# Causal mask of the row maxima on the diagonal: one TensorE matmul and a plain maximum in place of a masked VectorE pass

## What is computed

```python
xn = _layernorm(x)                                   # x: (1, 2048, 256)
k, q, v = einsum('ihd,bpd->biph', W_K / W_Q / W_V, xn)   # 16 heads of 128
scores = einsum('biph,biqh->biqp', k, q)
mask = tril(ones((pos, pos)))
masked = scores * mask - 1e10 * (1.0 - mask)
attn = softmax(masked / sqrt(128), axis=-1)
z = einsum('biqp,biph->biqh', attn, v)
s = einsum('df,bqf->bqd', W_O, z_flat)
g = silu(ffn(xn))            # base linear layer and one of 8 low-rank experts for each token
out = x + s * g
```

## Time and profile before

| | |
|---|---|
| median of 3 runs | 1450.78 us (1450.16 to 1451.8) |
| the profiled execution | 1450.27 us, its span 1448.2 us |
| PE busy | 1412.4 us, 98% of the span |
| DVE busy | 1191.9 us, 82% |
| ACT busy | 1086.5 us, 75% |
| POOL busy | 829.3 us, 57% |
| chain that ended last | PE 94% |

### The profile page before, as it was taken

The page is one execution under the profiler, slowest core; times in us unless marked ns, Lnnn a source line. Parts: engine busy times, 40 slices in busy tenths (PEclk is TensorE's granted clock), DMA queues, the critical chain, the costliest instruction groups (busy, mean ns, idle before and its releaser), DMA issues.

```text
span 1448.2 us, 23330 instructions
## 1 busy us (share of the span) xinstructions
PE 1412.4 (98%) x7788; PEld 1197.4 (83%) x7788; DVE 1191.9 (82%) x2541; ACT 1086.5 (75%) x2260; POOL 829.3 (57%) x688
## 2 busy tenths in 40 slices
PE   5899999999999999999999999999999999999996
PEld 4688888888888888888888888888888888888775
DVE  6679897798878987788977988789887898779964
ACT  2578886878778787788868787787877888688842
POOL 3265674556566474656745566555746567455840
PEclk9799999999999999999999999999999999999998
DMA  2110001010100101100010001001011000100002
GB/s 80 30 30 16 13 10 45 8 19 12 30 23 9 23 9 30 30 16 10 14 44 9 15 16 30 23 8 23 8 31 30 16 8 16 38 11 16 16 30 87
DMA packets 30072, 33.75 MB, mean 23 GB/s; under 512 B 11009, under 2 KB 17665, under 8 KB 29953
## 3 DMA queue, kind: packets, MB, share of 16 engines
q1 hardware_dynamic: 29952, 32.26, 9.3%
HBM read 30.02 MB, written 2.23 MB: 22 GB/s over the span
## 4 chain that ended last, share of the span: by engine, by line
PE 94%; DVE 2%; POOL 1%; DMA 1%; ACT 1%; issue 1%; SPq 0%; POOLq 0%; DVEq 0%; ACTq 0%
PE ps L293 27%; PE ps L294 26%; PE ps L295 26%; PE ps L745 9%; PE ps L780 3%; PE ps L757 1%; POOL colsum L446 1%; DMA acc<-x_dram 1%; DVE p_lo L577 1%; PE ps L808 1%; PE ps L698 0%; DVE acc L569 0%; PE ps L714 0%; DMA spread<-max_dram 0%; ACT p_hi L525 0%
## 5 line engine op out<-in xcount | busy, mean ns | idle before, releaser
L446 POOL TENSOR_TENSOR colsum<-colsum,probs 128x512 f32<-128x512 f32 (+3 forms) x512 | 643.6, 1257 | 240.6 <-ACT probs L524 208.0
L577 DVE TENSOR_TENSOR p_lo<-probs,p_hi 128x512 fp32r<-128x512 f32 (+3 forms) x640 | 561.9, 884 | 5.4 <-ACT p_hi L525 3.1
L524 ACT ACTIVATE probs<-ps 128x512 f32<-128x512 f32 (+3 forms) x640 | 344.8, 539 | 207.7 <-PE ps L295 123.3
L501 ACT ACTIVATE ps<-maxrow 128x512 f32<-128x512 f32 (+3 forms) x640 | 354.1, 553 | 0.0
L525 ACT ACTIVATE p_hi<-ps 128x512 fp32r<-128x512 f32 (+3 forms) x640 | 344.7, 539 | 0.0
L592 DVE TENSOR_REDUCE partmax<-ps 128x1 f32<-128x512 f32 x384 | 254.3, 681 | 7.6 <-PE ps L745 7.6
L293 PE MATMUL ps<-qT_hi,kT_hi 128*128 128x512 f32 (+3 forms) x640 | 239.7, 375 | 3.7 <-ACT ps L501 3.5
L293 PE MATMUL ps<-p_hi,v_hi 128*128 128x512 f32 (+3 forms) x640 | 238.0, 372 | 1.8 <-DVE p_lo L577 1.8
L294 PE MATMUL ps<-qT_lo,kT_hi 128*128 128x512 f32 (+3 forms) x640 | 233.3, 365 | 0.0
L295 PE MATMUL ps<-p_hi,v_lo 128*128 128x512 f32 (+3 forms) x640 | 233.1, 364 | 0.0
L295 PE MATMUL ps<-qT_hi,kT_lo 128*128 128x512 f32 (+3 forms) x640 | 232.8, 364 | 0.0
(11 more groups left out here) (107 smaller groups left out, 2247.1 us busy)
## 6 DMA issues: line engine op xcount, KB each, us to landing
spread<-max_dram SPq DMA_DIRECT2D x64, 256.0 KB, 3.8
wraw<-wqk_dram SPq DMA_DIRECT2D x16, 256.0 KB, 4.1
acc<-x_dram SPq DMA_DIRECT2D x4, 512.0 KB, 7.2
wraw<-wv_dram SPq DMA_DIRECT2D x8, 256.0 KB, 4.8
wraw<-wo_dram SPq DMA_DIRECT2D x8, 256.0 KB, 3.4
probs<-x_dram SPq DMA_DIRECT2D x4, 512.0 KB, 4.6
out_dram<-acc SPq DMA_DIRECT2D x4, 512.0 KB, 3.0
max_dram<-rowmax SPq DMA_DIRECT2D x64, 2.0 KB, 1.4
```

What stands on the lines that cost most here:

```text
L446: nc.gpsimd.tensor_tensor(total[:, c0:], total[:, c0:], tile[:, c0:], ALU.add)\
L501: nc.scalar.activation(st[job.n % SCORE_BANKS][:, c0:], maxrow[:, job.g, c0:], ACT.Copy)\
L524: nc.scalar.activation(probs[:, k, c0:], src, ACT.Exp, scale=SCALE).then_inc(probs_ready, 1)
L577: nc.vector.tensor_tensor(p_lo[:, k, c0:], probs[:, k, c0:], f32(p_hi[:, k, c0:]), ALU.subtract)\
```

## The change

The masked pass is replaced. On TensorE, after the matmul of a diagonal row maximum, a bfloat16 matmul with `mask_bf` stationary and `ident_bf` moving adds the transposed triangle to the last 128 columns of the bank, and the semaphore `aux_full` is raised by it and not by the matmul ahead of it. On VectorE every row maximum is now the same plain `reduce_max`, over the `w` columns where it is diagonal. The memset, the custom pass, its accumulator read, the tiles `mask_rows` and `wait_slot` and the view `masked_row` go, and on GpSimd the two instructions that made `mask_rows` go, ahead of `ones_r`. The list of the schedule is the same.

```diff
             nc.gpsimd.memset(mask_bf[:, :], 0.0).then_inc(made, 1)
-            nc.gpsimd.memset(mask_rows[:, :], 0.0).then_inc(made, 1)
             nc.gpsimd.memset(zeros[:, :], 0.0)
...
-            nc.gpsimd.affine_select(out=mask_rows[:, BW - P:], in_=mask_rows[:, BW - P:], compare_op=ALU.is_ge,
-                                    fill=MASKED, base=0, pattern=[[-1, P]], channel_multiplier=1)
             nc.gpsimd.tensor_copy(ones_r[:, :], ones[:, :]).then_inc(consts, 1)
...
                     dve.wait_ge(aux_full, job.aux + 1)
-                    if job.c < job.g:
-                        nc.vector.reduce_max(dst, src, axis=AX).then_inc(aux_free, 1)
-                    else:
-                        w = P * (job.q + 1)
-
-                        k = job.aux % AUX_BANKS
-                        nc.vector.memset(wait_slot[:, k:k + 1], 0.0)
-                        nc.vector.tensor_tensor_reduce(
-                            out=masked_row[:, k, 0:w], in0=src[:, 0:w], in1=mask_rows[:, BW - w:], scale=1.0,
-                            scalar=-3.0e38, op0=ALU.add, op1=ALU.max, accum_out=dst).then_inc(aux_free, 1)
+                    w = P * (job.q + 1) if job.c == job.g else BW
+                    nc.vector.reduce_max(dst, src[:, 0:w], axis=AX).then_inc(aux_free, 1)
...
                     w = P * (job.q + 1) if job.c == job.g else BW
-                    nc.tensor.matmul(dst[:, 0:w], qT_hi[:, job.g, job.q * P:(job.q + 1) * P],
-                                     kT_hi[:, k_slot(job.head, job.c), 0:w], start=True, stop=True)\
-                      .then_inc(aux_full, 1)
+                    op = nc.tensor.matmul(dst[:, 0:w], qT_hi[:, job.g, job.q * P:(job.q + 1) * P],
+                                          kT_hi[:, k_slot(job.head, job.c), 0:w], start=True, stop=job.c < job.g)
+                    if job.c == job.g:
+
+                        op = nc.tensor.matmul(dst[:, w - P:w], mask_bf[:, :], ident_bf[:, :], start=False, stop=True)
+                    op.then_inc(aux_full, 1)
```

More of the change, by code:

```diff
@@ L200, in attention_layer @@
         mask_bf = sb("mask_bf", [P, P], BF16)
-        mask_rows = sb("mask_rows", [P, BW])
         zeros = sb("zeros", [P, P])
-        wait_slot = sb("wait_slot", [P, AUX_BANKS])
         ones = sb("ones", [P, P])
@@ L213, in attention_layer @@
         gate = sb("gate", [P, 2, TB, D])
-        masked_row = gate[:, :, :, :].rearrange("p a t d -> p (a t d)")[:, 0:AUX_BANKS * BW]\
-            .rearrange("p (k n) -> p k n", k=AUX_BANKS)
         ps = ctx.enter_context(nc.psum_tensor("ps", [P, 8, BW], F32))
@@ L411, in _ @@
                 nc.gpsimd.memset(rank[:, :, e:e + 1], float(E - e))
-            pool.wait_ge(made, 5)
+            pool.wait_ge(made, 4)
             diagonal = dict(compare_op=ALU.not_equal, base=0, pattern=[[-1, P]], channel_multiplier=1)
```

## The result

The changed kernel takes 1476.4 us (median of 4 runs, 1475.85 to 1476.86), the kernel before 1450.47 us beside it: a ratio of 1.0178, 95% interval 1.0162 to 1.0194, 25.9 us more. The profiled execution took 1476.02 us, its span is 1474.0 us, so against the profiled execution of before (1450.27 us) it is 25.75 us. The forecast was 26.9 us more, 1477.2 us.

What follows compares the result with a forecast made beforehand. TensorE's full list was taken to set the time: 27.5 us for 256 added matmuls, less 0.9 us for eight early ones, plus 0.3 us at the start, gave 26.9 us more, 1477.2 us; range 1468 to 1483 us.

Steps and rivals of the forecast that it cites:

- The bound: In the long stretch TensorE issues matmuls one after the other, so whatever is put into its list is paid in full.
- The price behind a wide matmul: Behind row maxima of 256, 384 and 512 columns each added mask costs 0.12 us: 192 of them, 23.0 us.
- Width 128: Behind row maxima of 128 columns each added mask costs 0.07 us more: 64 of them, 4.5 us.
- The start: Eight masks before 48 us, where TensorE is not the bound, may delay the chain: +0.3 us, between -1.1 and +1.9 us.
- VectorE: Dropping accumulator reads and memsets frees 0 to 35.7 us on VectorE, counted as 0 in time, from -5 to +3 us.
- (a): The mask's weights load ahead, so each mask costs only its 128 columns, 0.06 us: 1465.6 us in all; chance 8%.
- (b): The mask waits until the row maximum's last columns are written, paying up to 0.23 us each: 1509 us; chance 5%.
- (c): VectorE's return of the three auxiliary banks sets TensorE's pace, so its saving counts: 1441.5 us at the full saving; chance 4%.
- (d): VectorE gains nothing from the plain maxima; the time is the forecast's, so it has no chance of its own.

Runs made afterwards that it cites:

- experiment 1: The changed kernel without the added matmul, so diagonal row maxima run unmasked: 1450.23 us against 1450.53 us for the kernel before, a ratio of 0.9997.
- experiment 2: The kernel before with the added mask matmul and its masked VectorE pass kept: 1476.29 us, a ratio of 1.0173 to the kernel before.
- experiment 7: From experiment 1, the score masks leave TensorE too; GpSimd adds the triangle and ScalarE seeds diagonal tiles: 1432.97 us against 1451.11 us for the kernel before.
- experiment 4: The changed kernel with the mask and identity of the added matmul in float32r: 1475.48 us, a ratio of 1.0169 to the kernel before.
- experiment 5: The changed kernel with the added matmul over the last 64 columns instead of 128: 1476.02 us, a ratio of 1.0166 to the kernel before.
- experiment 3: The changed kernel with the mask matmul issued twice in a row: 1489.53 us, a ratio of 1.0263 to the kernel before.
- experiment 6: The changed kernel with every diagonal maximum on VectorE taken twice: 1508.4 us, a ratio of 1.0385 to the kernel before.

## Why the prediction was right

**The bound.** That TensorE issues without a pause in the long stretch and everything put into its list is paid there: shown by experiments 1 and 2, whose times are those of the kernel before and of the changed one to within 0.3 us. The reverse does not hold as fully: experiment 7 took 256 masks off the list and got 18.1 us of the 28 back, because waits then came to light.

**The price behind a wide matmul.** 0.12 us was read from the score's mask and is what the added one costs. The exchanged operands changed nothing. The reason given beside it, a load that is not taken ahead, was true as a row but is the reason for 0.01 to 0.02 us at most: where the load is taken ahead (experiment 4), the price is 0.11 us. It is the load behind the mask that counts. The step survived because the number came from the distance of starts, which holds the whole cost whatever its cause.

**Width 128.** 0.07 us expected, 0.06 us at the place shown. With 0.107 us as the mean of 160, the 27.5 us for all 256 are confirmed (256 × 0.107 = 27.4). That the two agree so closely is in part luck: the prediction read 0.12 and 0.13 us at two places and took the lower, and the places of the changed kernel show up to 0.13 us, of which shorter gaps elsewhere give a little back. The 1 us by which the forecast of 26.9 us is too high lies outside the stretch from tile 80 to tile 480: the 40 masks ahead of tile 80 cost 220.30 - 217.02 = 3.28 us, and the 56 behind tile 480 the rest, 25.75 - 3.28 - 17.06 = 5.41 us, less than 0.107 us each in both.

**The start.** +0.3 us was a guess between -1.1 and +1.9. The second join of maxima on VectorE and the transfers behind it, in the changed kernel (DVE in order of time; the chain):

```profile
41.35 0.16 DVE L584 TENSOR_REDUCE rowmax<-partmax 128x4 f32<-128x8 f32 x1
```
```profile
42.97 4.16 DMA spread<-max_dram
...
48.80 0.80 PE ps L285
```

The transfer begins 0.05 us earlier than in the earlier trace rows and takes 0.17 us longer by itself; the first score matmul comes at 48.80 instead of 48.68 us. What the eight masks cost there can't be told from this: the same matmul starts at 49.12 us in experiment 1, which has no added masks, at 49.06 us in experiment 2 and at 48.07 us in experiment 5, which have them. Single executions differ by more than the term, so it is neither confirmed nor refuted.

**VectorE.** Counted at 0 with -5 us as the other end: it was 0 (ratio 0.9997). The bound of 35.7 us was far off, since the two small instructions overlap the passes; the busy time fell by 1.8 to 3.8 us. Its waits for TensorE did lengthen, as the prediction feared. Ahead of the plain maxima they are 14.3 us, where the earlier trace rows has 7.6 us. Ahead of the diagonal ones they are 8.8 us, 23 times, where the earlier trace rows has 5.9 us, 16 times, with no releaser named. TensorE's own waits for the maxima, the third row, are 4.4 us, no more than the 3.3 + 1.8 us of the earlier trace rows, so it cost nothing:

```profile
DVE partmax L581 <- PE ps L726: 14.3, 41, 0.6
...
DVE partmax L581 <- PE ps L730: 8.8, 23, 0.5
...
PEld ps L726 <- DVE partmax L581: 4.4, 12, 0.6
```

**The rivals.** (a), a mask for its columns alone, falls with the 0.12 us at L730 and with experiment 5, where half the columns save nothing. The 81 ns that the Trainium skill gives for each matmul in a stream of loads and matmuls of 128 columns ("TensorE: Matmul & The Clock Gate", "Back-to-back issue gap") is not what this stream shows; between two bfloat16 matmuls experiment 3 shows 0.051 us, and between a bfloat16 and a float32r one 0.12 us. (b), a wait for the columns just written, falls with the mask that starts 0.06 us behind a row maximum of 128 columns at 433.81 us. The prediction's row against it did not show as much: the 0.11 us of the earlier trace rows are later than the 0.06 us of the earlier trace rows. (c), a pace set by VectorE's return of banks, falls with experiment 1; experiment 6 shows that the banks do count once VectorE has 96 us more to do. (d), no gain on VectorE, is what happened.

## What to carry to other kernels

Price an added matmul by the distance from its start to the second start behind it, at a place where the trace already has the same kind between the same neighbours; its own duration and the first distance both mislead. In this stream, where every matmul brings new float32r weights, a short matmul costs the load of the weights behind it and not its columns, so with TensorE full it paid to move the masks to engines with room (18.1 us in experiment 7, not the 28 us that the price promised). And check that the pass to be relieved is dearer than its replacement: here masked and plain maxima took the same time.

## What the runs showed of the hardware

A custom VectorE pass that reads a bank and a mask row, writes a row and keeps a maximum takes as long as a plain maximum of the same width (684 and 682 ns at 512, 284 and 281 ns at 128). A bfloat16 weight load between float32r matmuls starts with its matmul (409.73 and 409.74 us, and so at all 256 masks of the changed kernel), a float32r one a matmul ahead (408.69 and 408.81 us). Behind a short matmul the next load follows a float32r load after 0.11 to 0.12 us (experiments 3 and 4, and the changed kernel), where one more bfloat16 matmul of 128 columns costs 0.051 us. A VectorE pass over SBUF alone can swallow time freed elsewhere: with the same list, the `p_lo` passes were 39.2 us longer where the maxima were shorter. GpSimd works in SBUF at the same time: in the kernel before, the 62 of the 448 passes of 512 columns that overlap no GpSimd instruction take 0.66 to 0.69 us, the other 386 take 1.06 us in the mean and up to 1.79 us. So the overlap goes with the longer passes; no run took GpSimd's work away to show it as the cause.
